# Causal attention on one core: all maxima of the last units two units ahead, and their shift turned in the second half step of the unit before

## The reference, cut to what matters

```python
scores = jnp.einsum('bhsd,bhtd->bhst', q, k) / scale
causal = jnp.tril(jnp.ones((S, S), dtype=bool))
scores = jnp.where(causal[None, None], scores, -jnp.inf)
attn = jax.nn.softmax(scores.astype(jnp.float32), axis=-1).astype(x.dtype)
out = jnp.einsum('bhst,bhtd->bhsd', attn, v)
```

## Time and profile before

| what | value |
|---|---|
| median of 3 runs | 1641.64 us (1635.99 to 1641.96) |
| the profiled execution's own time | 1640.22 us |
| its span, first to last instruction | 1638.5 us |
| TensorE busy, share of the span | 89% |
| VectorE busy | 71% |
| ScalarE busy | 64% |
| granted TensorE clock, mean | 0.923 |

### The profile page before, as it was taken

One profiled execution on the slowest core, in us unless ns is written; L12 is line 12 of the kernel. 1 busy time (PEld: TensorE's weight loads), 2 busy tenths in 40 slices (PEclk: granted clock), 3 DMA queues, 4 the chain that ended last, 5 costly groups with the idle time before them and its releaser, 6 DMA issues. The chain is left out here.

```text
span 1638.5 us, 30725 instructions
## 1 busy us (share of the span) xinstructions
PE 1458.2 (89%) x11729; PEld 651.8 (40%) x11729; DVE 1167.8 (71%) x1556; ACT 1045.4 (64%) x1992; POOL 226.5 (14%) x310
## 2 busy tenths in 40 slices
PE   6689999999988999686899999999999999983874
PEld 3233334444435444342333333333333333342773
DVE  6889878868535111349999999999999998346223
ACT  2247888888753222222488888888888888851552
POOL 4001112113230000120000000000000000001774
PEclk9579999999978999775699999999999999995998
DMA  4300000000000000120000000000000000004444
GB/s 151 111 1 8 8 8 8 15 8 14 14 2 1 1 0 0 60 71 13 0 8 8 8 8 8 8 8 8 8 8 8 2 1 1 1 1 128 124 143 138
DMA packets 34285, 45.91 MB, mean 28 GB/s; under 512 B 6000, under 2 KB 18749, under 8 KB 33631
## 3 DMA queue, kind: packets, MB, share of 16 engines
q1 hardware_dynamic: 29535, 38.76, 7.7%
q0 software_dynamic: 2496, 4.21, 0.9%
q10 hardware_dynamic: 2112, 1.05, 0.3%
HBM read 36.06 MB, written 8.85 MB: 27 GB/s over the span
## 5 line engine op out<-in xcount | busy, mean ns | idle before, releaser
L639 DVE TENSOR_REDUCE maxp<-banks 128x2 f32<-128x1024 f32 (+1 forms) x800 | 942.0, 1200 | 114.4 <-PE banks L483 64.1
L622 ACT ACTIVATE probs<-banks 128x512 f32<-128x512 f32 x1568 | 841.9, 596 | 167.2 <-PE banks L509 123.7
L528 PE MATMUL banks<-probs,V 128*9 128x256 f32 (+3 forms) x6016 | 482.3, 395 | 3.8 <-POOL probs L586 2.8
L509 PE MATMUL banks<-Q,K 64*128 64x512 f32 (+3 forms) x1664 | 435.2, 480 | 12.6 <-ACT probs L622 9.3
L483 PE MATMUL banks<-K,Q 64*128 64x512 f32 (+3 forms) x1664 | 381.1, 432 | 36.3 <-DVE maxp L639 29.9
L509 PEld LDWEIGHTS banks<-Q,K 64*128 64x128 f32 x1664 | 179.3, 185 | 369.6 <-ACT probs L622 317.2
L483 PEld LDWEIGHTS banks<-K,Q 64*128 64x128 f32 x1664 | 181.0, 198 | 82.6 <-DVE maxp L639 71.0
L528 PEld LDWEIGHTS banks<-probs,V 128*9 128x9 f32 x6016 | 91.3, 88 | 242.3 <-ACT probs L622 184.1
L572 POOL CAST Q<-Q 32x512 fp32r<-32x512 f32 x64 | 38.9, 607 | 703.0 <-ACT Q L610 580.8
L822 PE MATMUL banks<-work,flex 128*128 128x512 f32 x256 | 110.5, 592 | 0.0
L610 ACT ACTIVATE Q<-banks 32x512 fp32r<-32x512 f32 x64 | 37.7, 589 | 89.7 <-PE banks L468 88.6
(11 more groups left out here) (157 smaller groups left out, 914.9 us busy)
## 6 DMA issues: line engine op xcount, KB each, us to landing
ew<-in_down SPq DMA_DIRECT2D x39, 256.0 KB, 2.8
Q<-q_rows SPq DMA_DIRECT2D x256, 32.0 KB
tables<-in_tables SPq DMA_DIRECT2D x2, 2048.0 KB, 8.9
q_rows<-qb SPq DMA_DIRECT2D x8, 512.0 KB, 2.8
up_all<-in_up SPq DMA_DIRECT2D x1, 2064.0 KB, 12.1
flex<-in_h SPq DMA_DIRECT2D x2, 1024.0 KB, 7.1
x<-in_x SPq DMA_DIRECT2D x4, 256.0 KB, 3.9
xn_rows<-xn SPq DMA_DIRECT2D x1, 1024.0 KB, 6.1
```

The costliest lines, as they stand in the source:

```text
L509: mm = pe.matmul(ebank(e)[:, at:at + CW - low], k.K[rows, 2 * g + block, kt * P:(kt + 1) * P], k.Q[rows, n % Q_RING, block, low:CW], start ...
L528: mm = pe.matmul(acc[32 * j:32 * j + HD + 1, low + a:low + z], k.V9[:, kt, g * HG + j, :], k.probs[:, tile, at + a:at + z], start=(s == 0) ...
L622: act.activation(k.probs[:, number % 8, :], ebank(e), ACT.Exp, scale=scale).then_inc(e_done, 1)
L639: dve.tensor_reduce(dst, src, AX.X, ALU.max).then_inc(m_done, 1)
```

## The change

For units 13, 14 and 15 (`early`), all six reductions are done two units ahead instead of two of six; so unit 11 gets ten reductions instead of six, units 12 and 13 keep six each, now spread over the five half steps as two, one, one, one, one, and unit 14 has none. The shift of units 13, 14 and 15 is turned in half step 1 of the unit before, not in half step 3, on all engines that take the position from `shift_at`. VectorE does the three steps that make the shift of such a unit at the start of its segment, ahead of the reductions. The plan's rule that holds slots 0 and 1 to urgent reductions no longer applies where there are none. Nothing else changes, and no operation is added or removed.

```diff
-    ahead = [len(reductions(n)) * 3 // 8 if n != 1 else 4 for n in range(NU)]
+    early = [causal and n > 0 and units[n][0] == 0 and units[n - 1][0] == 0 for n in range(NU)]
+    ahead = [len(reductions(n)) if early[n] else len(reductions(n)) * 3 // 8 if n != 1 else 4 for n in range(NU)]
...
-    shift_at = [len(halves[n]) - (2 if causal else 3) for n in range(NU)]
+    shift_at = [1 if n + 1 < NU and early[n + 1] else len(halves[n]) - (2 if causal else 3) for n in range(NU)]
...
-            if slot < 2:
+            if slot < 2 and urgent:
                 enough = min(enough, urgent)
...
                 before_shift = sum(len(slot) for slot in plan(n + 1)[:shift_at[n + 1]]) if -1 <= n < NU - 1 else len(todo)
+                while n + 2 < NU and early[n + 2] and follow:
+                    follow.pop(0)()
                 for i in range(len(todo) + 1):
```

## The result

The changed kernel took 1620.39 us, median of 4 runs (1619.4 to 1623.05), against 1641.8 us (1635.99 to 1641.98) beside it: a ratio of 0.9885, 95% interval 0.9868 to 0.9903. It is faster by 21.4 us in the medians, and by 16 to 22 us as the interval has it. Predicted were 1628.1 us and 1624 to 1636.

A forecast was written before the change was run, and what follows sets the result against it. A chain of waits, no full engine, bounds units 12 to 14: 38.93 us less 26.3 gains 12.6, less 0.5 in unit 11 gives 12.1; 1640.2 - 12.1 = 1628.1 us, range 1624 to 1636.

The forecast's parts named there:

- The hand-overs: Engine-to-engine waits in units 12 to 14, eight a unit at 0.05 to 0.15 us; 0.6 us a unit taken.
- the chain: Units 12 to 14, counted from first scores through exponentials, shift copy and masks: 8.3 us with six maxima, 7.95 without.
- the clock's return behind the attention: Stages behind the attention: nothing in the sum, 1.7 us either way in the range for where the clock recovers.
- The bound: Units 12 to 14, 38.93 us together: a chain of waits with no engine full, the clock falling three times.
- a fall at each such wait: Units 12 to 14: at each wait for VectorE the clock falls to 0.50 for 6.7 to 6.8 us.
- Unit 11: Four more reductions cost 1.1 us, less a 0.63 us wait: 0.5 us longer, between nothing and 0.8.
- Its stream: TensorE's work at full clock in a unit with six maxima: 7.5 us; without maxima 4.8 us.
- Unit 14: Has no maxima after the change; its chain ends at 7.95 us, with the last mask done at 6.95.
- the favourable bound: Upper bound of the gain: 38.93 us less 25.7 for units 12 to 14, with unit 11 free, 13.2 us.
- Unit 15: Took 8.22 us before, 1.1 us of it at half clock; used to check unit 14's size, no gain summed.
- The clock did not fall in units 14 and 15: Rival: the clock falls once or twice in units 14 and 15, giving 1630.6 to 1633.1 us; chance 0.20.
- VectorE was not the bound: Rival: VectorE's reductions delay maxima and shift by 1.5 to 2 us in units 12 and 13; 1631.5 us, chance 0.08.

The follow-up runs named there:

- The kernel with the interleaved steps: The changed kernel with VectorE's three shift steps between the next reductions in units 12 and 13, not ahead of them; 1645.70 us against 1661.85 for the kernel before.
- the twice-issued maxima: The kernel before with the maxima matmuls of units 12 to 14 issued twice; 1659.39 us, ratio 0.9985 to the kernel before.
- the delay: The changed kernel with seven unused VectorE reciprocals added in the norm behind the first attention; 1648.21 us against 1661.85 for the kernel before.
- the second profile of before: The kernel before, run again unedited for its profile; units 12 to 14 took 37.5 us, the stage behind the attention 33.8 us.
- the version between: The changed kernel with unit 15's last two reductions back in unit 14 and all shifts turned in half step 3; 1645.13 us against 1661.85 for the kernel before.
- The repeats: The changed kernel timed twice more, unedited, against the kernel before: ratios 0.9915 and 0.9894.
- second repeat: The changed kernel, unedited, timed once more against the kernel before; 1625.68 us against 1640.61, ratio 0.9894.
- bunched: The changed kernel with the six reductions of units 12 and 13 as three each in slots 0 and 1; 1650.41 us against the changed kernel's 1646.08.
- first repeat: The changed kernel, unedited, timed again against the kernel before; 1646.08 us against 1662.64, ratio 0.9915.

## Why the prediction was right in kind and too small

The profiled execution took 1623.05 us, 5 us less than the forecast 1628.1. The hand-overs, which I had added to the chain, are 1.7 us of it, unit 11 0.4, unit 15 0.3; the clock's return behind the attention, which stood at nothing in the sum, is 2.1, and 0.5 lies elsewhere. The median lies another 2.7 us lower.

*The bound.* Right in the main: a chain of waits for VectorE, with the clock falling behind it. The kernel with the interleaved steps brings both back; the twice-issued maxima put the clock's share at 2.1 us or more of unit 13, the waits' at up to 3.05. Two readings were off. The slice where the last units lie reads seven tenths in the earlier trace rows, the twelfth, not nine. And a fall at each such wait is too strong a rule: there are waits without a fall and falls without such a wait.

*Unit 11.* Forecast 0.5 us longer, measured 0.10. The work was sized rightly, TensorE's busy time grew by 1.12 us where I had 1.1, and the wait of 0.63 us before its shift went. So did a wait of 0.51 us for one of ScalarE's banks, at 429.74 in the kernel before, which I had not counted; the added maxima fill it.

*Stream and chain in units 12 and 13.* The chain gave 8.3 us before any addition; measured 8.27 and 8.28. The shift was ready 1.2 us into the unit, as forecast, the turn came at 1.73 us (forecast 1.85), the fourth half step's second scores ran from 4.8 to 5.3 us (5.0 to 5.2). My reading that ScalarE's chain alone sets these units was wrong: turning the shift in half step 3 changes that chain and leaves the pair at 16.55 us. TensorE, busy for 8.05 us, fills them; in unit 13 it idles 0.18 us for ScalarE's bank at 457.07 and then works without a gap to the end. Its stream had been put at 7.5 us. GpSimd's last mask ended at 459.53, only 0.05 us before TensorE came to the values that need it, so the chain's number for the whole unit fits the stream's partly by luck.

*Unit 14.* The chain gave 7.95, measured 8.04. Here the place of the shift copy on ScalarE does set the time: TensorE waits 0.55 us for it, the exponentials behind it are late, and moving the turn back gives 6.96.

*Hand-overs: the term that was mis-sized.* I added 0.6 us a unit, 1.8 us in all, taken from one gap of 0.15 us at a wait that itself was to go. Measured, they are worth nothing on top: 24.59 us against the bare chain's 24.55. The 0.59 us from scores to exponential and the start-to-start times run from one start to the next, so a hand-over between them is already inside; I counted it twice. Even the favourable bound had 1.2 us of hand-overs in it, which, with the 0.3 us of unit 15, is why the attention's 14.55 us lie beyond my 13.2.

*Unit 15.* Not in my sum, though I had written that 1.1 us of its 8.22 were at half clock. At full clock it takes 7.93: 0.3 us.

With 1.7 (for the three units) + 0.4 (unit 11) + 0.3 (unit 15) us these bring the forecast 12.1 us to the 14.5 that the attention gained.

*Behind the attention.* I had allowed 1.7 us either way for where the clock recovers and put nothing into the sum. It gave 2.1 us in this comparison, 34.3 us from the output stage's first matmul to the first hidden-layer matmul before and 32.2 after, and the delay shows that this follows the clock and not the work. Against the second profile of before it is 1.6 us. That it fell on the side of a gain is luck as far as the runs show: a kernel as close to the changed one as the version between did not have it. With 0.5 us elsewhere, that is the 17.2 us between the two spans.

*The rest.* The medians differ by 21.4 us, 4 us more than the spans. The repeats, with 16.6 and 14.9 us, put this down to how executions fell in the first comparison: the same kernel's single runs lie 10 to 12 us apart in them. The shorter runs are mostly those with the higher mean granted clock: in the second repeat 1616.5 and 1617.8 us at 0.931 and 0.932, the other four 1624.9 to 1628.9 at 0.923 to 0.927; in the first comparison 1619.4 to 1620.7 at 0.930 to 0.932, the profiled one 1623.05 at 0.928. My range had 1 us for this. With the bare chain and unit 11 free (14.4 us), the clock's 2 us and some 4 us of the runs' spread, its lower end comes to 1640.2 - 20.4, about 1620 us, not 1624; that spread is known only from the repeats.

*The rivals.* The clock did not fall in units 14 and 15 of the changed kernel in any of four profiles (the delayed kernel's is the fourth), and VectorE was not the bound as long as its work was spread; bunched, its reductions were part of a cost of 2.1 us a unit. The Trainium skill's rule (TensorE: Matmul & The Clock Gate, A second HAM failure mode: psum-queue depth-cycling), that frequent short idling of TensorE between groups of matmuls makes the clock go up and down, is not borne out by the changed kernel, whose units keep 1.00; the kernel with the shift in half step 2 fits it, with 0.71 and 0.59 in units 14 and 15.

## What to carry to other kernels

When a chain is built from start-to-start times of a trace, the hand-overs are in them; add none unless a row shows one on the new path. Moving work earlier can gain by two ways that look like one: the result is ready in time, and the work no longer comes in a bunch. A version that undoes one of them tells them apart, and it has to restore the old bunch exactly to size its share. Where the clock fell in the norm's pause, the same work behind it took 32.1 to 34.3 us, by when the clock came back; a swing of that size belongs in the range of every change ahead of it.

## What the runs showed of the hardware that was not expected

The routed-experts stage at the end took 152.2 us in the changed kernel's first profile and 172.5 us in the profile of the same kernel's first repeat, on another chip, with the clock at 0.83 and 0.77 and the same instructions. From the gate's first matmul to the end:

```profile
1469.10:1621.30 152.20, 91.30 (x729) 85.45 (x729) 56.09 (x193) 58.81 (x198) 82.13 (x82) 0.83 0.48 143
```

```profile
1467.80:1640.30 172.50, 105.14 (x729) 97.42 (x729) 55.73 (x193) 59.37 (x198) 81.37 (x82) 0.77 0.44 126
```

That is about all of the 20 us by which the medians were longer there, while units 12 to 14 agree to 0.02 us. The stage, which no version touches, falls in two groups over the twelve profiles: 150.9 to 154.4 us in the four where before took about 1641 us, 171.1 to 174.4 in the eight where it took about 1662. Why it is slower on some chips is open. The 3.5 us from the shortest to the longest within one group, of a kernel before and a changed kernel on the same chip, is also a reason why medians can differ by more or less than the attention's 14.5 us.
